# Attention rebuilt: stacked query and key parts, turned scores, stationary values, outputs turned per batch

## What is computed

```python
h = layernorm(x)                                    # (4, 512, 128)
q, k, v = heads(h @ Wq), heads(ctx @ Wk), heads(ctx @ Wv)   # 16 heads of 8
s = q @ k.T * scale[l] + mask[l]                    # (4, 16, 512, 77)
x = x + tanh(g_xattn[l]) * (softmax(s) @ v @ Wo)
x = x + tanh(g_ffn[l]) * ffn[l](layernorm(x))
```

## Time and profile before

| | us |
|---|---|
| runs | 961.72, 963.01, 969.97 |
| median | 963.01 |
| the profiled execution, first to last instruction | 960.8 |

### The profile page before, as it was taken

One profiled execution on the slowest core, in us unless ns is written; L12 is line 12 of the kernel. 1 busy time (PEld: TensorE's weight loads), 2 busy tenths in 40 slices (PEclk: granted clock), 3 DMA queues, 4 the chain that ended last, 5 costly groups with the idle time before them and its releaser, 6 DMA issues.

```text
span 960.8 us, 13366 instructions
## 1 busy us (share of the span) xinstructions
PE 767.5 (80%) x4914; PEld 592.3 (62%) x4914; DVE 664.4 (69%) x1496; ACT 301.0 (31%) x548; POOL 236.8 (25%) x539
## 2 busy tenths in 40 slices
PE   3685787456559999986898991289998899999998
PEld 2474666344447777764677771167777677777775
DVE  3967987698875576649777774956665766757554
ACT  2242343221214433432333540135344322222211
POOL 3633421244550141137334322401211000000000
PEclk9697998676779999999799995579999799999999
DMA  6650000000000000001010000000001000000000
GB/s 139 36 76 1 1 1 1 0 1 0 1 0 1 1 1 1 1 1 62 1 50 2 1 1 1 0 1 1 1 1 51 1 1 1 12 1 12 1 12 12
DMA packets 51195, 11.68 MB, mean 12 GB/s; under 512 B 44108, under 2 KB 50316, under 8 KB 50748
## 3 DMA queue, kind: packets, MB, share of 16 engines
q1 hardware_dynamic: 51132, 10.84, 6.1%
HBM read 9.16 MB, written 1.68 MB: 11 GB/s over the span
## 4 chain that ended last, share of the span: by engine, by line
PE 58%; DVE 28%; issue 6%; ACT 4%; POOL 2%; DMA 1%; SPq 0%; DVEq 0%
PE ps L1099 14%; PE ps L1281 8%; PE ps L1064 6%; PE ps L1072 5%; PE ps L1086 4%; DVE xn L670 4%; PE ps L1259 3%; PE ps L1261 3%; PE ps L1260 3%; DVE mx L702 3%; ACT pt L473 3%; DVE pq L705 3%; PE ps L1270 2%; PE ps L1115 1%; DVE st L656 1%
## 5 line engine op out<-in xcount | busy, mean ns | idle before, releaser
L1099 PE MATMUL ps<-vb,pt 128*128 128x144 f32 x1280 | 175.4, 294 | 11.5 <-DVE loT L692 9.6
L1099 PEld LDWEIGHTS ps<-vb,pt 128*128 128x128 f32 x1280 | 167.5, 197 | 14.3 <-issue 14.1
L473 ACT ACTIVATE pt<-ps 128x512 f32<-128x512 f32 (+1 forms) x192 | 94.1, 524 | 145.3 <-PE ps L1086 142.9
L702 DVE TENSOR_REDUCE mx<-ps 128x8 f32<-128x616 f32 x128 | 101.5, 793 | 20.7 <-PE ps L1072 19.0
L496 ACT ACTIVATE pq<-pq 128x616 f32<-128x616 f32 x128 | 88.1, 712 | 82.6 <-DVE pq L705 82.3
L1086 PE MATMUL ps<-ident,pq 128*128 128x128 f32 x640 | 99.1, 290 | 15.2 <-ACT pt L473 15.2
L705 DVE TENSOR_TENSOR pq<-ps,mx 128x616 f32<-128x616 f32 x128 | 102.3, 800 | 4.4
L713 DVE RECIPROCAL rd<-ps 128x16 f32<-128x16 f32 x64 | 16.4, 256 | 116.6 <-PE ps L1099 116.5
L1086 PEld LDWEIGHTS ps<-ident,pq 128*128 128x128 f32 x640 | 74.8, 147 | 33.4 <-ACT pt L473 30.3
L955 DVE TENSOR_TENSOR pq<-ps,pq 128x512 f32<-128x512 f32 x72 | 49.8, 691 | 64.2 <-ACT pq L566 57.0
L381 POOL TENSOR_TENSOR nt<-nhv,rs 128x4 f32<-128x4 f32 x108 | 24.4, 226 | 279.5 <-DVE rs L663 273.4
(11 more groups left out here) (223 smaller groups left out, 1298.3 us busy)
## 6 DMA issues: line engine op xcount, KB each, us to landing
mst<-in_moe_gate SPq DMA_DIRECT2D x1, 1152.0 KB, 4.9
mst<-in_moe_up SPq DMA_DIRECT2D x1, 1152.0 KB, 5.0
pt<-in_moe_down SPq DMA_DIRECT2D x1, 1152.0 KB, 5.1
x<-in_x SPq DMA_DIRECT2D x4, 256.0 KB, 6.1
out<-x SPq DMA_DIRECT2D x4, 256.0 KB, 2.3
wp<-in_wp SPq DMA_DIRECT2D x1, 704.0 KB, 4.0
v_bounce<-vs SPq DMA_DIRECT2D x4, 154.0 KB
m1f<-in_m SPq DMA_DIRECT2D x1, 616.0 KB, 5.1
```

Source lines behind the costliest of these rows:

```text
L473: act.activation(pt[:, t % 2, 4 * r:4 * r + w, :], ps[:, 4 + R % 2, 0:w * P].rearrange("p (c q) -> p c q", q=P), ACT.Copy).then_inc(evac_d ...
L702: link(dve.tensor_reduce(m, sc, AX_X, ALU.max))
L1099: ins = pe.matmul(ps[:, 6, 0:VW], pt[:, t % 2, c, :], vb[:, n % 2, c, :, :].rearrange("p h e -> p (h e)"), start=c == 0, stop=c == NC - 1)
```

## The change

It rebuilds attention and what feeds it; the feed-forward blocks compute what they did.

- **Scores** for a group are one product: `KG` holds high, low and high keys stacked on rows 0 to 95, `QG` high, high and low queries. SP fills both by DMAs from SBUF to SBUF, 12 for keys and 12 for queries a batch (`keys`, `queries_in`). For layer 3 the mask lies on rows 96 and 97.
- **Scores are computed twice.** By token (128 tokens x 308 columns) only for the maximum (`scores`, DVE `maximum`, 308 numbers each). POOL splits the maxima, PE turns them, ACT copies, SP writes them in 4 DMAs to rows 98 to 105 of `QG` (`maxima_in`). A second product, by key (`turned_scores`: up to 110 keys x 512 tokens), has the maximum subtracted by those rows and -1 in `KG`. ACT exponentiates it from PSUM (`weigh`). No subtraction on DVE and no transposes of weights are left.
- **Values are stationary** (`weighted_sum`): `VN` of up to 110 rows and 36 columns, with `PT` of 512 tokens as moving operand in F32, 12 a batch, written to output rows 0 or 64 in turn. 6 DMAs a batch fill `VN` (`values`).
- **Outputs are turned per batch:** two times four transposes of the sums, DVE `normalise` on halves, four transposes, `project`.
- Masks of layers 1 and 2 are added by products with `rep`/`repb`, to both kinds of scores: two F32R ones in layer 1, a bf16 one in layer 2.
- **Order:** a loop over `k` = -2..4 and 12 steps `c`. PE does the scores of batch k+1 while it weighs batch k. All of layer l's work on PE waits for the block before to be fully read. The loads at the start are ordered anew.

```diff
+            def keys(n):
+                if n >= 3:
+                    sp.wait_ge(st_ps, NCH * (n - 2))
+                sp.wait_ge(km_ready, n + 1)
+                for g in range(G):
+                    r = slice(32 * g, 32 * g + 32)
+                    sp.dma_start(KG[0:32, n % 3, g, :].bitcast(F32), kmH[r, n % 2, :].bitcast(F32)).then_inc(kg_in[n % 3], 16)
+                    sp.dma_start(KG[32:64, n % 3, g, :].bitcast(F32), kmL[r, n % 2, :].bitcast(F32)).then_inc(kg_in[n % 3], 16)
+                    sp.dma_start(KG[64:96, n % 3, g, :].bitcast(F32), kmH[r, n % 2, :].bitcast(F32)).then_inc(kg_in[n % 3], 16)
...
+            def queries_in(n):
+                sp.wait_ge(q_hi, n + 1)
+                sp.wait_ge(q_lo, n + 1)
+                if n >= 3:
+                    sp.wait_ge(st_ps, NCH * (n - 2))
...
+            def maxima_in(n):
+                sp.wait_ge(mT_ready, n + 1)
+                for g in range(G):
+                    sp.dma_start(QG[98:106, n % 3, g, :].bitcast(F32), mT[32 * g:32 * g + 32, n % 2, :].bitcast(F32)).then_inc(mg_in[n % 3], 16)
...
+                for k in range(-2, B):
+                    if k + 2 < B:
+                        queries_in(l * B + k + 2)
...
+                    if 0 <= k + 1 < B:
+                        maxima_in(l * B + k + 1)
...
+                    if k >= 0 and l * B + k + 3 < N:
+                        keys(l * B + k + 3)
+                        values(l * B + k + 3)
```

ACT and DVE:

```diff
+                def weigh(b, c):
+                    q = (l * B + b) * NCH + c
+                    w = CH[c // G][1]
+                    act.wait_ge(st_ps, q + 1)
+                    if q >= 4:
+                        act.wait_ge(pv_done, q - 3)
+                    act.activation(PT[0:w, q % 4, :], ps[0:w, 4 + q % 2, :], ACT.Exp, scale=SCALE[l]).then_inc(exp_done, 1)
...
+                for k in range(-2, B + 1):
+                    for c in range(NCH):
+                        if 0 <= k < B:
+                            weigh(k, c)
+                        if c == 0 and k + 2 < B:
+                            xT_one(k + 2)
+                        if c == (3 if k >= 0 else 1) and k + 2 < B:
+                            q_one(k + 2)
+                        if c == 10 and 0 <= k + 1 < B:
+                            maxima_out(k + 1)
...
+                    dve.tensor_reduce(mraw[:, n % 2, i, g * HG:(g + 1) * HG],
+                                      ps[:, u % 2, 0:GK].rearrange("p (h k) -> p h k", k=K), AX_X, ALU.max).then_inc(max_done, 1)
...
+                if l == 2:
+                    weight8_magnitude()
+                    inner_norm_residual(3)
+                for k in range(-2, B + 1):
+                    for c in range(NCH):
+                        if c == (3 if k >= 0 else 0) and k + 2 < B:
+                            q_rest(k + 2)
+                        if c == 0:
+                            after(k, c)
+                        if c < 8 and 0 <= k + 1 < B:
+                            for u in (2 * c, 2 * c + 1):
+                                maximum(k + 1, u // G, u % G)
+                        if c in (3, 5) and k >= 1:
+                            normalise(k - 1, (c - 3) // 2)
+                        if c > 0:
+                            after(k, c)
+                    if k >= 1:
+                        residual_read(k - 1)
+                        residual(k - 1)
```

`after` holds the normalising of whole batches (c = 0, 8, 9) and in layer 0 the quantising (c = 9, 10). PE:

```diff
+CH = [(0, 110), (110, 88), (198, 110)]
+VC = 36
+KS, KZ = 98, 106
+LAG = 2
...
+                    if u >= 2:
+                        pe.wait_ge(max_done, u - 1)
+                    o = ps[:, u % 2, 0:GK]
+                    ins = pe.matmul(o, QG[0:KS, n % 3, g, q], KG[0:KS, n % 3, g, :], start=True, stop=l not in (1, 2))
+                    if l == 1:
+                        hi, lo = m1_of(b)
+                        pe.matmul(o, hi[:, b % 2, q], rep[:, :], start=False, stop=False)
+                        ins = pe.matmul(o, lo[:, b % 2, q], rep[:, :], start=False, stop=True)
...
+                    if c == 0:
+                        pe.wait_ge(mg_in[n % 3], 64 * uses(n))
+                    if q >= 2:
+                        pe.wait_ge(exp_done, q - 1)
+                    o, r = ps[0:w, 4 + q % 2, :], slice(r0, r0 + w)
+                    ins = pe.matmul(o, KG[0:KZ, n % 3, g, r], QG[0:KZ, n % 3, g, :], start=True, stop=l not in (1, 2))
...
+                    pe.wait_ge(exp_done, q + 1)
+                    p0 = 64 * (g % 2)
+                    pe.matmul(ps[p0:p0 + VC, 6 + g // 2, :], VN[0:w, n % 3, g * 3 + j, :], PT[0:w, q % 4, :],
+                              start=j == 0, stop=j == 2, skip_group_check=True).then_inc(pv_done, 1)
...
+                for k in range(-2, B + 1):
+                    for c in range(NCH):
+                        if c == 0 and k + 2 < B:
+                            turn_input(k + 2)
+                        if c == (3 if k >= 0 else 0) and k + 2 < B:
+                            queries(k + 2)
+                        if c < 8 and 0 <= k + 1 < B:
+                            for u in (2 * c, 2 * c + 1):
+                                scores(k + 1, u // G, u % G)
+                        if 0 <= k < B:
+                            turned_scores(k, c)
+                            if c >= LAG:
+                                weighted_sum(k, c - LAG)
+                        if c in (2, 4) and k >= 1:
+                            turn_sums(k - 1, (c - 2) // 2)
+                        if c == 6 and k >= 1:
+                            att_transposed(k - 1)
+                        if c == 8 and k >= 1:
+                            project(k - 1)
+                        if c == 10 and 0 <= k + 1 < B:
+                            turn_maxima(k + 1)
+                    if 0 <= k < B:
+                        for c in range(NCH - LAG, NCH):
+                            weighted_sum(k, c)
```

More of the change, by code:

```diff
@@ L279, in _ @@
+            for n in range(2):
+                keys(n)
+                values(n)
+            next_mask(0)
+            keys(2)
+            values(2)
+            sp.dma_start(m3f[:, :, :], a["m3"].partition_broadcast(P)).then_inc(ld_const, 16)
+            sp.dma_start(repb[:, :], a["repb"]).then_inc(ld_const, 16)
             sp.dma_start(w1s[:, :], a["w1"]).then_inc(ld_ffn1, 16)
@@ L1030, in turn_input, with queries @@
                     ins.then_inc(xT_ps, 1)
[L1032 removed]
+                def queries(b):
                     pe.wait_ge(xT_ready, nT(2 * l, b) + 1)
[L1034 to L1040 removed]
@@ new lines, in turn_sums @@
+                def turn_sums(b, h):
+                    n = l * B + b
+                    pe.wait_ge(o_out, 2 * n + h + 1)
+                    if h == 1:
+                        pe.wait_ge(att_done, 2 * n + 1)
+                    elif n >= 1:
+                        pe.wait_ge(y_done, n)
+                    for i in range(TPB):
+                        ins = pe.transpose(ps[:, 3, i * P:i * P + 100], o_sb[0:100, h, i * P:(i + 1) * P], ident[0:100, 0:100])
+                    ins.then_inc(oT_ps, 1)
@@ L1111, in project, with att_transposed @@
+                def att_transposed(b):
+                    n = l * B + b
+                    pe.wait_ge(att_done, 2 * n + 2)
+                    for i in range(TPB):
+                        ins = pe.transpose(ps[:, 3, i * P:(i + 1) * P], att[:, i, :], ident[:, :])
+                    ins.then_inc(attT_ps, 1)
                 def project(b):
@@ L1313, in layout @@
     r = np.arange(P)
-    flat = np.arange(NC * P)
-    owner = np.where(flat < HK, flat // K, -1)
-    e = np.arange(NE)
+    owner = np.arange(GK) // K
+    turned = np.arange(GK) % K
+    vn = np.zeros((110, NCH, VC), f)
+    for h, k0, k1, j, r0 in RUNS:
+        for g in range(G):
+            vn[r0:r0 + k1 - k0, g * 3 + j, HG * DH + h] = 1
     a = dict(
```

769 lines of the change are left out of this document (396 added, 373 removed).

## The result

| | before | after |
|---|---|---|
| median of the runs, us | 966.49 (4 runs, 961.72 to 971.08) | 1162.36 (4 runs, 1155.57 to 1175.27) |
| span of the profiled execution, us | 960.8 | 1161.1 |
| mean granted TensorE clock in it | 0.89 | 0.739 |

The ratio is 1.200, with a 95% interval of 1.191 to 1.209. Medians count every run of a kernel, while ratios leave out those over 1.5% above its lowest, here the one of 1175.27. I said 1025, in a range of 960 to 1060, with slower at 0.76. The direction was right. The size wasn't: 63 us of loss were forecast and 196 came.

What follows compares the result with a forecast made beforehand. PE was taken to set the pace in layers 1 to 3, with DVE having more to do in layer 0. Layers 0 to 3 at +2, +32, +22 and +7 us gave +63 on 960.8, stated as 1025; range 960 to 1060.

Steps and rivals of the forecast that it cites:

- The low clock after the idle start: Layer 3's loop: score pairs slower at first (0.62 against 0.41), costing an estimated 2 us.
- The first rival (no drain): Weighted sum shares a mode with its neighbours, so 69 us go and the kernel ends at 956; chance 0.12.
- A step of 1.43: Loop on PE: turned score 0.213, weighted sum 0.86 and two mode changes 0.36 together; twelve steps 17.0 us.
- The loop's stalls: Layer 3's loop: PE waits 3.4 us at c = 3 and 3 us at the starts of k = 1..3.
- The wait at c = 3: With k = 0 or 1, scores 8 waits for maximum 6 behind `q_rest`: 1.7 us twice, 3.4.
- The waits for the maxima's transfer: Start of k = 1..3: maxima travel 4.8 us against 4.0 of cover, scores then at DVE's pace; 3 us.
- The start, 21 us: Before a layer's first turned score: issues and landing 7.7, 16 maxima 7.9, split and transfer 5.4; PE nearly idle.
- The end, 7 us: Behind the last weighted sum: copies, transposes, DVE operations and projection, 7 us.
- SP's issues: SP's DMA queue: 0.47 us an issue, 34 issues or 16.6 us a batch, hidden while rounds last 21 or more.
- SP becomes the bound: At 0.6 us an issue, 20.4 a batch, rounds and prologues grow; kernel at 1045 to 1065; chance 0.17.
- the forecast's drains: Array drains at two mode changes beside every weighted sum in the loops: 0.36 us a step, 69 us over all.
- the signs that I named: Trace signs: step starts 1.4 or 1.9 us apart, PE near idle 20 us at starts with low clock, 34 issues.

Runs made afterwards that it cites:

- experiment 1: Changed kernel with the weighted sum's weights zero-padded from 36 columns: to 100 or 72 without its mode change, 1032.78 and 1036.49 us; to 64 with it, 1161.92.
- 100 columns: Changed kernel with the weighted sum's 36 columns of weights zero-padded to 100, written from column 0 without a mode change: 1032.78 us, ratio 1.070.
- experiment 5: Kernel padded to 100 columns with SP relieved, order and starts mended; last edits (layer 0's start, two maxima issues on ACT): 950.17 us, in one FP32R pass 946.83.

## Why the prediction was right in direction and wrong in size

- **The clock.** "The low clock after the idle start (...) costs an estimated 2": this is the step that failed. I took the low clock as a matter of the start and priced it at 2 us for the whole loop. In layer 3's loop 0.74 means, by the two levels, that about half of it ran at the low one; PE's work takes twice as long there (1.86 against 0.98 for a sum), so by an estimate that counts all of the loop as PE's 113 x 0.26 = 29 us are lost, not 2. What remains, 84, is close to the loop forecast without that term, 92. In layers 1 and 2, at 0.71 and 0.66, the misses are 32 and 43 us. I had read that PE would be busy throughout and taken that for a held clock. I didn't weigh that PE, counted as busy, may stream nothing while it changes mode. That the mode changes bring most of the low clock is shown by experiment 1 (0.74 to 0.90); by what means they do is not. The first rival (no drain) had the right lever but, by my sum, would have given 956; the run without drains gave 1033.
- **A step of 1.43.** Measured 1.31 at the high level. Turned score 0.23 and weighted sum 0.86 were right. The changes cost 0.10 and 0.12 instead of 0.18 each, close to the 0.10 of the earlier trace rows. The other 0.08, which I had inferred from what a whole expert step leaves over, didn't carry over.
- **The loop's stalls.** The wait at c = 3 was forecast at 1.7, twice. It is 1.46, twice, in layer 3 of the changed kernel and up to 1.58 with 100 columns, and undoing it was part of 30 us. The waits for the maxima's transfer, forecast at 3, come to 2.1 and 2.9 ahead of the last two rounds.
- **The start, 21 us.** Measured 24.9: 9.0 (7.7) for issues and landing, 9.9 (7.9) for the maxima, which run at 0.60 each at the low level, 5.9 (5.4) for split, turn and transfer. **The end, 7 us**, took 6.7.
- **SP's issues.** From the earlier trace rows I took 0.47, and 0.6 for many small rows. SBUF to SBUF they come 0.63 apart, 0.75 for maxima and 0.86 for values: 23.4 us a batch and not 16.6. The rival "SP becomes the bound" was nearer on the price (20.4) and wrong on the place. In the rounds SP hardly binds: relieving it shortened those of layers 0 and 3 by at most 1.7 us. It binds in the starts, and in layer 0, where the first score came at 73.9 and not at 58.5. That layer was forecast at +2 and measured at +40, a miss of 38, next to 43 in layer 2, 31 in layer 1 and 23 in layer 3.
- **Check by the kernel without mode changes.** Taking the forecast's drains (17 a layer) off its own sums gives 105 us for layer 3, 142 for layer 1, 123 for layer 2 and an end of layer 0 at 163. With 100 columns they are 118, 155, 134 (and 8 at its start instead of 5) and 196. That is 13, 13, 14 and 33: 73 of the 77 us between 956 and 1033. In layer 3 it is 4.7 at the start (25.7 from the start of `loT` to the first turned score) and some 9 by the clock in the loop (88 x 0.10). Layer 0 adds the issues.
- **Range.** It ended at 1060 because SP was the worst case that I had worked out. No case had a clock below that of the profile I read, though I was putting more idle time beside PE in every part, and none of the signs that I named looked at the clock inside the loop.

## What to carry to other kernels

Read the granted clock by stage, and when a change puts pauses beside TensorE (mode changes, an idle start, waits), price its remaining work at both levels and keep the low one in the range. Work taken off TensorE in a stage that something else also holds may come back as waits and a lower clock: one pass in place of two took 17 us of busy time out of a loop and made it 8 us shorter. A product of few columns of weights between full ones is cheaper padded with zeros, here by 129 us of 1162, and if it must stay narrow, two of them in different columns belong next to each other.

## What the runs showed of the hardware that I had not expected

- TensorE busy for 104.9 of 113 us by the records, with two mode changes a step, ran at a mean of 0.74 of its clock. Padding the same products with zeros gave 0.90.
- 48 fewer passes in layer 1, in FP32R, left PE's busy time longer (138.0 against 134.4 us) in the one execution profiled, at a clock of 0.63 against 0.85. After the last edits of experiment 5 the same step made that layer's loop 5 us shorter (104 against 108), at 0.77 against 0.97.
- Two f32 sums of 36 columns of weights, at array columns 0 and 64, take 1.86 us together at the low level when adjacent, as long as one, and 0.99 at the high level.
- An SBUF to SBUF issue holds SP's queue for 0.59 us, one for the strided values 0.83, one from DRAM 0.43; from ACT's queue the values take 0.84 in the median.
- Eleven products of 512 columns that nobody reads raised a layer's clock from 0.85 to 0.90 and didn't change the kernel's time.
